# A chain of transformer blocks on one core, with the fillers of TensorE's waits taken out

## The chip, the cores and the metric

The kernel runs on one NeuronCore of a Trainium2 chip. It is written by hand for the five engines: TensorE (PE, matrix products; its weight loads are PEld), VectorE (DVE), ScalarE (ACT), GpSimd (POOL) and SyncE (SP, which issues the DMAs). The metric is the device time of one execution in microseconds (us), of which the median of some runs is taken. Changes under about 0.3% can't be told from none.

## The reference

Four blocks follow each other. Each takes the output of the last as x, of shape 4 x 512 x 256 (batch, sequence, width), and a context of the same shape. Cut to what is computed:

```python
# L0: 16 heads of 64, softmax over the QUERY axis, rows masked by mask[b, q]
q, k, v = x @ WQ.T + bQ, ctx @ WK.T + bK, ctx @ WV.T + bV
A = where(mask[:, None, :, None] == 0, -inf, q @ k^T / 8)
x0 = softmax(A, axis=2) @ v @ WO.T + bO + x
# L1: a gate from the pooled context, three iterations of which the last one counts, LayerNorm
# L2: 16 heads of 16, relu on Q, K, V, key mask and causal mask, relu on the output,
#     residual, normalised with the standard deviation over n - 1
# L3: self-attention (16 heads of 16, window of 64, linear bias by head), residual, LayerNorm;
#     cross-attention to ctx (no mask), residual, LayerNorm;
#     gelu(x @ w1 + b1) @ w2 + b2 (inner width 1024), residual, LayerNorm
```

## The kernel before, in words

A hardware loop runs over the four batch elements. One iteration computes all blocks for one element; I call the iterations b0 to b3. Every engine has its own program, and semaphores order them. Each engine runs its instructions in the order written, so a wait holds up all that is behind it on that engine.

TensorE writes into a ring of three PSUM slots of two banks (`ring`) and into `obank`, two banks for the products of probabilities and values. All uses of the ring stand in one list of jobs, `JOBS`; `start(name)` waits until the slot of the job has been drained, and the last matmul of a job increments `filled`. Who drains (VectorE or ScalarE) increments `drained`.

The jobs of an iteration that matter here, in TensorE's order:

- `V0`, `QK0`, `S0`: the 16 heads of 64 of block L0 (lines 1060 to 1088), then its output product (L1144) and block L1 (`tp`, `gate`, `agree`, with the matmuls of one column L1206 and the gate products L1162).
- `VC` (L1041): values of the cross-attention. Then `X1`: `turn(1)` transposes the normalised tiles `nat_n` (L1116), four tiles of two transposes. A tile is ready when VectorE has normalised it (L833, semaphores `tile_normed` and `norm_ready`). ScalarE drains the slot into `act_t` (L630 or L633).
- `Q2` (L1029), then `meanV` (L1222, sixteen matmuls of one column) and `meanO` (L1229).
- `attention(CAUSAL)` and its output product `O2` (L1327).
- `X2`, then `KS`, `QS` (L1029), `VS` (L1041), `attention(BANDED)`, `KC`, `OS`.
- `X3`, then `QC` (L1029), `attention(FULL)`, `OC`.
- `X4`, then `F1` (L1029) and `F2` (L1050). A product of 128 rows and 512 columns in fp32 is one instruction of the program and two in the trace, so F1 has 32 there.

An attention works on four groups of four heads. In the pass A (`pass_a`, L1251, for CAUSAL and BANDED with mask products L1237) scores are made with the queries on the partitions, and VectorE takes their maxima (L912). `turn_maxima` (job `T`, L1298) turns the maxima of a group, and ScalarE copies them into the query tiles (L673, two copies). Then pass B (L1268) makes the scores with the keys on the partitions, ScalarE takes the exponentials (L681), and `values` (L1287) multiplies them into `obank`. The first eight A passes of group 0 come before everything else; `group_steps` interleaves all that follows.

The query and key tiles of an attention are stacked by small DMAs, 24 for the keys (L381) and 24 for the queries (L388), which SyncE issues one after the other. The first pass A waits for the stacked tiles of its group (L1246). Before the queries are stacked, VectorE drains the projection in halves (L902), ScalarE rounds each (`high_q`, L623) and VectorE subtracts (L905). For the keys GpSimd makes the lower parts (`split_k`, L507).

Between the real work stand calls of `keep_warm(n)` (L1022). Each issues n products of two constants that stay in SBUF, a 128x128 identity and 512 columns, in bf16, into bank 0 of `obank` at times when that bank holds nothing. Nobody reads them, and they wait for nothing of their own. They stand behind the start of X1 (12), X2, X3 and X4 (18 each), behind each of these four (5), at the start of an attention (6), behind each of the eight first passes of FULL (2), behind the first eight passes (8), and before the first pass B (6): 162 in one iteration.

## Time and profile before

| | us |
|---|---|
| median of 3 runs | 1832.75 (1827.45 to 1833.13) |
| the profiled execution | 1834.59 |
| its span | 1832.5 |
| TensorE busy | 1615.1 (88%) |
| VectorE busy | 914.4 (50%) |
| ScalarE busy | 737.6 (40%) |
| GpSimd busy | 251.8 (14%) |

The span goes from the first to the last instruction of the profiled execution. Busy is the time in which an engine has an instruction under way; a matmul's record contains the time in which it passes through the array, so that records of neighbours overlap and a busy TensorE isn't one at its peak. "Granted clock" is the share of TensorE's full clock (2.4 GHz) that the chip let through; in a short stretch it is 1.00 or 0.50, and over a longer one the mean of both. In timelines, x12 is the number of instructions merged into one row, and the brackets hold the engine's idle time before them and what ended it.

### The profile page before, as it was taken

The numbers are of one execution on the slowest core, as the hardware profiler recorded it, in microseconds if no ns is written. First come the engines' busy times: TensorE is split into PE (matmuls) and PEld (weight loads), VectorE is DVE, ScalarE is ACT, GpSimd is POOL, SyncE is SP. The second block draws the span as 40 slices with busy tenths as digits, with TensorE's granted clock in tenths as the row PEclk, the third lists the DMA queues.
The fourth block names the chain that finished last, engine by engine and source line by source line (L and its number), as shares of the span: only waits on it lengthen the run. The fifth ranks groups of instructions, "written<-read, shape, count | busy, mean of one in ns | idle before, by whom it ended". The sixth has DMA issues, their size and how long they took to land.

```text
span 1832.5 us, 27225 instructions
## 1 busy us (share of the span) xinstructions
PE 1615.1 (88%) x9568; PEld 834.5 (46%) x9568; DVE 914.4 (50%) x2244; ACT 737.6 (40%) x1281; POOL 251.8 (14%) x116
## 2 busy tenths in 40 slices
PE   5999888888999988878999998887899999988786
PEld 2346445424435645532533554553253355545234
DVE  2653644472464474447166346445625635644561
ACT  1651434164264252417236316142724632514362
POOL 1012211201102121110110312111011031112102
PEclk9998998889999898889999989889999998988899
DMA  9001203402100211240210030224111013031300
GB/s 324 1 6 35 35 17 55 104 1 109 48 1 7 41 30 32 39 104 1 110 47 1 7 57 14 49 54 72 36 75 47 1 21 55 2 62 41 60 24 12
DMA packets 44869, 84.17 MB, mean 46 GB/s; under 512 B 10417, under 2 KB 28593, under 8 KB 44465
## 3 DMA queue, kind: packets, MB, share of 16 engines
q1 hardware_dynamic: 44288, 78.42, 18.2%
q10 hardware_dynamic: 432, 3.83, 0.5%
q8 instruction: 86, 1.41, 0.3%
q14 instruction: 63, 0.51, 0.1%
HBM read 42.37 MB, written 2.10 MB: 24 GB/s over the span
## 4 chain that ended last, share of the span: by engine, by line
PE 55%; issue 24%; DVE 8%; ACT 5%; POOL 4%; SPq 3%; DMA 1%; ACTq 0%; DVEq 0%; POOLq 0%
PE ring L1078 7%; PE obank L1088 7%; PE ring L1068 6%; PE ring L1029 5%; DVE nmax L912 4%; PE obank L1022 4%; PE ring L1144 3%; PE obank L1287 3%; PE ring L1327 3%; PE ring L1251 2%; SPq L381 2%; PE ring L1050 2%; ACT region_e L681 2%; PE ring L1268 2%; POOL q_all L528 2%
## 5 line engine op out<-in xcount | busy, mean ns | idle before, releaser
L912 DVE TENSOR_REDUCE nmax<-ring 128x2 f32<-128x1024 f32 (+4 forms) x384 | 318.2, 855 | 208.0 <-PE ring L1237 143.1
L681 ACT ACTIVATE region_e<-ring 128x1024 f32<-128x1024 f32 (+4 forms) x384 | 269.2, 732 | 140.9 <-PE ring L1237 87.3
L788 DVE CUSTOM_DVE_ANT_0 region_d<-ring,maskb 128x512 f32<-128x512 f32 x256 | 165.9, 687 | 101.1 <-issue 101.1
L605 ACT ACTIVATE region_e<-region_d,nmin 128x512 f32<-128x512 f32 x256 | 182.6, 714 | 81.8 <-DVE nmin L788 80.2
L673 ACT ACTIVATE q_all<-ring 2x1024 fp32r<-2x1024 bf16 x96 | 97.5, 1016 | 244.3 <-PE ring L1298 243.7
L1022 PE MATMUL obank<-cbf 128*128 128x512 bf16 x648 | 173.8, 412 | 0.0
L1237 PE MATMUL ring<-cbf 64*128 64x128 bf16 (+1 forms) x2048 | 168.2, 251 | 0.0
L1251 PE MATMUL ring<-k_tiles_a,q_all 64*128 64x512 f32 (+4 forms) x384 | 86.3, 457 | 65.5 <-DMA q_all<-q_parts 54.3
L1078 PE MATMUL ring<-region_q 64*128 64x512 f32 x512 | 126.1, 613 | 5.4 <-ACT region_q L594 5.4
L539 POOL TENSOR_TENSOR nat_x<-nat_n,rows 128x1024 f32<-128x1024 f32 x16 | 37.6, 2352 | 671.6 <-DVE nat_n L833 507.8
L1088 PE MATMUL obank<-region_e,vs 128*64 128x512 f32 x512 | 124.0, 605 | 0.0
L1251 PE MATMUL ring<-k_tiles_b,q_all 64*128 64x512 f32 (+4 forms) x384 | 81.9, 423 | 24.1 <-ACT q_all L673 15.1
L1022 PEld LDWEIGHTS obank<-cbf 128*128 128x128 bf16 x648 | 62.7, 103 | 82.6 <-issue 30.3
L1268 PE MATMUL ring<-q_all,k_tiles_a 64*128 64x512 f32 (+4 forms) x384 | 82.9, 427 | 18.7 <-DVE nmax L912 12.9
L1251 PEld LDWEIGHTS ring<-k_tiles_a,q_all 64*128 64x128 f32 x384 | 43.0, 221 | 103.7 <-DMA q_all<-q_parts 51.7
L1268 PE MATMUL ring<-q_all,k_tiles_b 64*128 64x512 f32 (+4 forms) x384 | 75.6, 412 | 13.1 <-ACT q_all L673 8.5
L1327 PE MATMUL ring<-w_out,region_d 128*128 128x256 f32 x384 | 85.7, 381 | 0.0
L514 POOL TENSOR_TENSOR q_all<-zero 128x2048 fp32r<-128x2048 f32 x8 | 28.6, 3598 | 404.0 <-DVE region_c L779 404.0
L1078 PEld LDWEIGHTS ring<-region_q 64*128 64x128 f32 x512 | 44.3, 186 | 84.8 <-issue 72.2
L1287 PE MATMUL obank<-region_e,region_b 128*32 128x192 f32 (+4 forms) x1024 | 81.7, 397 | 1.2 <-ACT region_e L681 0.8
L1287 PE MATMUL obank<-region_e,region_c 128*32 128x512 f32 x512 | 74.2, 654 | 7.0 <-ACT region_e L681 7.0
L983 DVE TENSOR_TENSOR nat_y<-ring,nat_x 128x512 f32<-128x512 f32 x16 | 11.1, 692 | 138.9 <-PE ring L1050 123.2
(169 smaller groups left out, 2260.9 us busy)
## 6 DMA issues: line engine op xcount, KB each, us to landing
q_all<-q_parts SPq DMA_DIRECT2D x288, 64.0 KB, 2.3
k_tiles_a<-k_parts SPq DMA_DIRECT2D x144, 64.0 KB, 2.3
k_tiles_b<-k_parts SPq DMA_DIRECT2D x144, 64.0 KB, 2.3
region_b<-in_w_f SPq DMA_DIRECT2D x8, 1024.0 KB, 5.2
wvo<-in_wv SPq DMA_DIRECT2D x4, 1024.0 KB, 7.8
wqk<-in_wq SPq DMA_DIRECT2D x4, 1024.0 KB, 11.0
wqk<-in_wk SPq DMA_DIRECT2D x4, 1024.0 KB, 12.9
wvo<-in_wo SPq DMA_DIRECT2D x4, 1024.0 KB, 5.4
```

Of the source, the lines that this page charges most:

```text
L605: ins = act.activation(e0[:, n % E0, h, :], sm0[:, n % 2, h, :], ACT.Exp, bias=nmin0[:, n, h:h + 1], scale=-1.0, accum_out=sum0[:, n, h:h ...
L681: act.activation(e16[:, n % 4, 2 * u:2 * u + 2, 0:nq], slot((a, "B", g, kt, u))[:, :, 0:nq], ACT.Exp)\
L788: ins = dve.tensor_tensor_reduce(out=sm0[:, n % 2, h, :], in0=slot(("S0", p, kt))[:, h, :], in1=maskb[:, :], scale=-1.0, scalar=3.0e38, op ...
L912: dve.tensor_reduce(nmax[:, qt, 2 * u:2 * u + 2], slot(name)[:, :, 0:nk], AX.X, ALU.max, negate=True)\
L1022: pe.matmul(obank[:, 0, :], cb("ident", P), cb("keyrows", S), start=True, stop=True)
L1078: ins = pe.matmul(dst[:, h, :], qk0[own, p % 2, 1, kt * P:(kt + 1) * P], qk0[own, p % 2, 0, :], start=True, stop=True)
L1088: ins = pe.matmul(obank[DK0 * h:DK0 * (h + 1), p % 2, :], vs0[:, n % 4, h, :], e0[:, n % E0, h, :], start=(kt == 0), stop=(kt == NT - 1))
L1237: ins = pe.matmul(dst[:, i, lo:lo + n], cb("halves", P, own, at=half * P), cb(table, n, own, at=half * whole + at), start=False, stop=(hal ...
L1251: ins = pe.matmul(dst[:, i, 0:nk], q_tiles[g][own, u, qt * P:(qt + 1) * P], k_tiles[g][own, u, k0:k0 + nk], start=True, stop=(a == FULL))
L1268: ins = pe.matmul(dst[:, i, 0:nq], k_tiles[g][own, u, kt * P:(kt + 1) * P], q_tiles[g][own, u, q0:q0 + nq], start=True, stop=(a == FULL))
L1287: ins = pe.matmul(obank[32 * s:32 * s + 32, (PAIRS + o) % 2, q0:q0 + nq], v_of[a][:, kt, h, :], e16[:, n % 4, s, 0:nq], start=(kt == 0), s ...
L1327: ins = pe.matmul(dst[j][:, i, 0:D], oT[:, t, m * P:(m + 1) * P], w_out[a][:, t, :], start=(t == 0), stop=(t == GROUPS - 1))
```

## The change

All calls of `keep_warm` and the function itself are deleted.

```diff
--- before.py
+++ after.py
@@ -1016,11 +1016,6 @@
                     pe.wait_ge(*free_for(name, b))
                     return slot(name)
 
-                def keep_warm(n):
-
-                    for _ in range(n):
-                        pe.matmul(obank[:, 0, :], cb("ident", P), cb("keyrows", S), start=True, stop=True)
-
                 def project(name, w, src, tiles):
 
                     dst = start(name)
@@ -1105,8 +1100,6 @@
                 def turn(n, src):
 
                     dst = start(("X", n))
-                    if n:
-                        keep_warm(12 if n == 1 else 18)
                     for m in range(NT):
                         if n and m + 1 < NT:
                             pe.wait_ge(tile_normed, (b * 5 + n - 1) * (NT - 1) + m + 1)
@@ -1209,7 +1202,6 @@
                 pe.wait_ge(k_loaded["lc"], 64)
                 project_nat("VC", w_sq["cv"], ctx_t)
                 turn(1, nat_n)
-                keep_warm(5)
                 pe.wait_ge(*drained_by(("X", 1), b))
                 project(("Q2",), w_sq["q2"], act_t, range(DT))
 
@@ -1299,20 +1291,14 @@
                     ins.then_inc(*ends_fill(name))
 
                 def attention(a):
-                    keep_warm(6)
                     for qt in range(NT):
                         for u in range(2):
                             pass_a(a, 0, qt, u)
-                            if a == FULL:
-                                keep_warm(2)
-                    keep_warm(8)
                     if a == BANDED:
                         pe.wait_ge(*drained_by(("VS", 1), b))
                         pe.wait_ge(ones_ready, b * 2 + 2)
                     for g in range(GROUPS):
                         for kind, *which in group_steps(g):
-                            if kind == "B" and which == [0, 0, 0]:
-                                keep_warm(6)
                             if kind in "ABTV":
                                 {"A": pass_a, "B": pass_b, "T": turn_maxima, "V": values}[kind](a, *which)
 
@@ -1335,7 +1321,6 @@
 
                 pe.wait_ge(k_loaded["ls"], 64)
                 turn(2, nat_n)
-                keep_warm(5)
                 pe.wait_ge(*drained_by(("X", 2), b))
                 project(("KS",), w_sq["sk"], act_t, range(DT))
                 project(("QS",), w_sq["sq"], act_t, range(DT))
@@ -1345,13 +1330,11 @@
                 project(("KC",), w_sq["ck"], ctx_t, range(DT))
                 out_heads(BANDED, "OS")
                 turn(3, nat_n)
-                keep_warm(5)
                 pe.wait_ge(*drained_by(("X", 3), b))
                 project(("QC",), w_sq["cq"], act_t, range(DT))
                 attention(FULL)
                 out_heads(FULL, "OC")
                 turn(4, nat_n)
-                keep_warm(5)
                 pe.wait_ge(*drained_by(("X", 4), b))
                 pe.wait_ge(k_loaded["ff"], b * 32 + 32)
                 for j in range(FT // 2):
```

No other instruction changes, so on TensorE each real instruction moves up by the fillers that stood ahead of it. Three places show it. Line numbers below 1016 stay, later ones fall by 5 to 18.

First TensorE between the values of the cross-attention and Q2. Before (L1022 are fillers, L1116 the transposes X1, L1029 is Q2; ISA and REGISTER_ALU rows are the computed waits):

```order
L1022 MATMUL obank<-cbf 128x512 x12
L1112 ISA
L1116 MATMUL ring<-ident,nat_n 128x128 x2
L1112 REGISTER_ALU
L1116 MATMUL ring<-ident,nat_n 128x128 x2
L1112 REGISTER_ALU
L1116 MATMUL ring<-ident,nat_n 128x128 x2
L1114 REGISTER_ALU
L1116 MATMUL ring<-ident,nat_n 128x128 x2
L1022 MATMUL obank<-cbf 128x512 x5
L1213 REGISTER_ALU
L1029 MATMUL ring<-act_t,w_q 128x512 x4
```

After (L1109 are the transposes, L1024 is Q2):

```order
L1036 MATMUL ring<-w_cv,ctx_t 128x256 x8
L1105 ISA
L1109 MATMUL ring<-ident,nat_n 128x128 x2
L1105 REGISTER_ALU
L1109 MATMUL ring<-ident,nat_n 128x128 x2
L1105 REGISTER_ALU
L1109 MATMUL ring<-ident,nat_n 128x128 x2
L1107 REGISTER_ALU
L1109 MATMUL ring<-ident,nat_n 128x128 x2
L1205 REGISTER_ALU
L1024 MATMUL ring<-act_t,w_q 128x512 x4
```

The transposes now stand right behind VC, and Q2 right behind the transposes.

Second TensorE from QC into the first A passes of FULL. Before (L1029 is QC, L1251 a pass A):

```order
L1029 MATMUL ring<-act_t,w_cq 128x512 x4
L1022 MATMUL obank<-cbf 128x512 x6
L1246 ISA
L1251 MATMUL ring<-k_tiles_a,q_all 128x512 x2
L1022 MATMUL obank<-cbf 128x512 x2
L1251 MATMUL ring<-k_tiles_a,q_all 128x512 x2
L1022 MATMUL obank<-cbf 128x512 x2
L1016 REGISTER_ALU
L1251 MATMUL ring<-k_tiles_a,q_all 128x512 x2
L1022 MATMUL obank<-cbf 128x512 x2
```

After (L1024 is QC, L1243 a pass A):

```order
L1024 MATMUL ring<-act_t,w_cq 128x512 x4
L1238 ISA
L1243 MATMUL ring<-k_tiles_a,q_all 128x512 x4
L1016 REGISTER_ALU
L1243 MATMUL ring<-k_tiles_a,q_all 128x512 x6
L1016 REGISTER_ALU
```

The passes stand behind each other with nothing between them but their waits for a drained slot.

Third TensorE at the end of FULL's first passes, up to the first pass B. Before (L1298 turns the maxima, L1268 is the first pass B):

```order
L1022 MATMUL obank<-cbf 128x512 x10
L1016 REGISTER_ALU
L1251 MATMUL ring<-k_tiles_a,q_all 128x512 x4
L1294 REGISTER_ALU
L1298 MATMUL ring<-cbf,mcol 128x128 x8
L1016 REGISTER_ALU
L1251 MATMUL ring<-k_tiles_a,q_all 128x512 x4
L1022 MATMUL obank<-cbf 128x512 x6
L1268 MATMUL ring<-q_all,k_tiles_a 128x512 x2
```

After (L1290 turns the maxima, L1260 is the first pass B):

```order
L1243 MATMUL ring<-k_tiles_a,q_all 128x512 x4
L1286 REGISTER_ALU
L1290 MATMUL ring<-cbf,mcol 128x128 x8
L1016 REGISTER_ALU
L1243 MATMUL ring<-k_tiles_a,q_all 128x512 x4
L1260 MATMUL ring<-q_all,k_tiles_a 128x512 x2
```

What stood between the eighth pass and the next, and between the last pass A and the first pass B, is gone. VectorE's, ScalarE's and SyncE's instructions are the same in both kernels.

## Rows read from the trace of the kernel before

**Rows 1.** View of the cores.
```profile
core 0: 1832.5 us, clock 0.937
```

**Rows 2.** The chain that ended last, by engine.
```profile
PE 55%; issue 24%; DVE 8%; ACT 5%; POOL 4%; SPq 3%; DMA 1%; ACTq 0%; DVEq 0%; POOLq 0%
```

**Rows 3.** Groups by cost: names, shapes, count, busy us, mean ns, idle before.
```profile
L1022 PE MATMUL obank<-cbf 128*128 128x512 bf16 x648 | 173.8, 412 | 0.0
```

**Rows 4.** Timeline of VectorE, X1 of b1: start us, us, what.
```profile
624.98 1.38 DVE L833 TENSOR_SCALAR nat_n<-nat_y,mv,std 128x256 f32<-128x256 f32 x4 [0.60 <-ACT std L643]
```

**Rows 5.** Timeline of TensorE, X1 of b1.
```profile
627.55 2.75 PE L1022 MATMUL obank<-cbf 128*128 128x512 bf16 x12
630.13 1.04 PE L1116 MATMUL ring<-ident,nat_n 128*128 128x128 f32 x8
```

**Rows 6.** Timeline of TensorE, X2 of b1.
```profile
707.18 1.65 PE L1116 MATMUL ring<-ident,nat_n 128*128 128x128 f32 x8 [1.98 <-DVE nat_n L833]
708.63 2.34 PE L1022 MATMUL obank<-cbf 128*128 128x512 bf16 x5
```

**Rows 7.** Timeline of ScalarE, X2 of b1.
```profile
708.87 1.02 ACT L630 ACTIVATE act_t<-ring 128x1024 f32<-128x1024 f32 x1 [2.61 <-PE ring L1116]
```

**Rows 8.** Timeline of TensorE before a first B: FULL b0, BANDED b1, FULL b2.
```profile
370.32 2.74 PE L1022 MATMUL obank<-cbf 128*128 128x512 bf16 x6
...
738.72 2.74 PE L1022 MATMUL obank<-cbf 128*128 128x512 bf16 x6
...
1275.23 1.47 PE L1022 MATMUL obank<-cbf 128*128 128x512 bf16 x6
```

**Rows 9.** Timeline of ScalarE at the same three places.
```profile
368.47 2.04 ACT L673 ACTIVATE q_all<-ring 2x1024 fp32r<-2x1024 bf16 x2 [20.78 <-PE ring L1298]
...
737.55 2.04 ACT L673 ACTIVATE q_all<-ring 2x1024 fp32r<-2x1024 bf16 x2 [17.96 <-PE ring L1298]
...
1273.46 2.04 ACT L673 ACTIVATE q_all<-ring 2x1024 fp32r<-2x1024 bf16 x2 [20.42 <-PE ring L1298]
```

**Rows 10.** Timeline of VectorE, first passes of FULL in b0.
```profile
357.99 1.23 DVE L912 TENSOR_REDUCE nmax<-ring 128x2 f32<-128x1024 f32 x1 [0.47 <-PE ring L1251]
359.68 6.88 DVE L912 TENSOR_REDUCE nmax<-ring 128x2 f32<-128x1024 f32 x6 [0.47 <-PE ring L1251]
```

**Rows 11.** Timeline of TensorE, first pass of FULL in b0.
```profile
355.46 0.80 PE L1251 MATMUL ring<-k_tiles_a,q_all 64*128 64x512 f32 x2 [7.92 <-DMA q_all<-q_parts]
```

**Rows 12.** Timeline of TensorE, X4 and F1 of b0.
```profile
435.77 1.41 PE L1116 MATMUL ring<-ident,nat_n 128*128 128x128 f32 x8
...
438.72 14.00 PE L1029 MATMUL ring<-act_t,region_b 128*128 128x512 f32 x32 [0.46 <-ACT act_t L633]
```

**Rows 13.** Timeline of TensorE, gate products of b1 at full and half clock.
```profile
607.74 1.13 PE L1162 MATMUL ring<-w_gt,region_q 128*128 128x256 f32 x4
...
614.54 2.08 PE L1162 MATMUL ring<-w_gt,region_q 128*128 128x256 f32 x4
```

**Rows 14.** Stretches, first pass to output product: CAUSAL b0, b1; FULL b0, b2.
```profile
core 0: us, PE busy (x) PEld busy (x) DVE busy (x) ACT busy (x) POOL busy (x), PEclk, DMA share, GB/s
193.38:252.41 59.03, 53.19 (x592) 30.50 (x591) 38.38 (x66) 29.73 (x40) 14.12 (x7) 0.97 0.12 21
643.55:701.16 57.61, 51.75 (x592) 29.84 (x592) 38.37 (x66) 29.79 (x40) 14.13 (x7) 1.00 0.12 21
...
355.46:431.88 76.42, 65.87 (x350) 25.30 (x351) 49.66 (x61) 39.49 (x40) 0.00 (x0) 0.88 0.21 60
...
1260.79:1333.05 72.26, 61.38 (x351) 24.41 (x352) 49.58 (x61) 39.49 (x40) 0.00 (x0) 0.95 0.22 64
```

**Rows 15.** Stretches from FULL's first pass while at half clock, b1 and b2.
```profile
808.03:813.80 5.77, 5.77 (x14) 1.55 (x14) 3.67 (x3) 0.00 (x0) 0.00 (x0) 0.50 0.58 101
...
1260.79:1264.40 3.61, 3.61 (x10) 1.07 (x10) 2.31 (x2) 0.00 (x0) 0.00 (x0) 0.50 0.61 104
```

**Rows 16.** Timeline of SyncE, query DMAs of FULL in b0.
```profile
349.93 15.14 SPq L388 DMA_DIRECT2D q_all<-q_parts  x24
```

**Rows 17.** Timeline of ScalarE, upper halves of FULL's queries in b0.
```profile
347.07 0.63 ACT L623 ACTIVATE q_parts<-region_e 128x512 fp32r<-128x512 f32 x1 [1.08 <-DVE region_e L902]
```

## The prediction

> **What bounds the kernel now.** First the view of cores: 1832.5 us, mean granted clock 0.937 [rows 1]. TensorE is granted either 2.4 or 1.2 GHz, so the share s of the span at 1.2 GHz follows from 1 - s/2 = 0.937: s = 0.126, about 231 us. Then the chain of waits by engine [rows 2]: 55% of the span is TensorE's own work, no other engine has more than 8%, and 24% is "issue", where the chain follows an engine that waits for nothing shown. So TensorE's stream is the backbone. Third, the groups by cost: the fillers are 648 matmuls, 173.8 us of busy time, with no idle time before them [rows 3]; 162 stand in each of the four loop iterations, which I call b0 to b3. Last, the timelines around each place with fillers. They sort the fillers into those that end before the next operand is there (free) and those that outlast it (paid). What both kinds may also do is keep the clock up.
>
> **What the removal gives back on the path.**
> (a) X1. The last tile of nat_n is ready at 626.36 (start 624.98 plus 1.38) [rows 4], before the twelve fillers start at 627.55; the transposes start behind them, at 630.13 [rows 5]. Nothing else is late then: 2.58 us in each iteration, 10.3 us. X1, Q2, the query DMAs and the first pass hang on it in a row.
> (b) X2. In b1 the five fillers start at 708.63 at half clock and take to about 710.8 [rows 6], while ScalarE has drained X2 at 709.89 [rows 7]: 0.9 us. So in b1, b2 and b3: 2.8 us.
> (c) Before the first B of an attention, six fillers. In BANDED they start at 738.72 at half clock, 2.7 us [rows 8], and ScalarE's two copies of the maxima end at 739.59 [rows 9]: 1.8 us late, in three iterations. In FULL of b0 the copies end at 370.51 and the fillers at 373.0: 2.5 us. At full clock six fillers take 1.4 us, to 1276.6 against copies that end at 1275.50: 1.1 us, three times [rows 8, 9]. CAUSAL has no such overhang. Sum 5.4 + 2.5 + 3.3 = 11.2 us.
> (d) FULL's first eight passes. VectorE needs 1.13 us start to start (the last six take 6.88), but the reductions at 357.99 and 359.68 stand 1.69 apart with 0.47 idle [rows 10], since at half clock a pass and its two fillers take TensorE 1.7 us. A pass alone takes it 0.8 at most [rows 11], so VectorE will set the pace: two times 0.56, about 1.1 us in each iteration, 4.5 us.
> Together 28.8 us. The 18 fillers ahead of X2, X3 and X4 give nothing back. At X2 TensorE idles another 1.98 us behind them [rows 6]; at X4, and alike at X3, they end as the first tile comes, with no idle time before the transposes [rows 12]. The fillers ahead of FULL's first pass end 7.92 us before the DMA that it waits for [rows 11].
>
> **What it costs in clock.** Prices first. For dense fp32 work the cost is all of it: four L1162 matmuls take 1.13 us at full clock and 2.08 at half [rows 13], so each us at half clock does half a us of work. In the attention phases VectorE and ScalarE share the bound, and the same phase in different iterations gives the price [rows 14]: CAUSAL 59.03 us at clock 0.97 against 57.61 at 1.00 is 1.42 us for 3.5 us at half clock, 0.40; FULL 76.42 at 0.88 against 72.26 at 0.95 is 4.16 for 11.1, 0.37, which I take for BANDED too. How long half clock lasts once work is back: in the four starts of FULL it ended after 3.6 to 5.8 us (both ends shown) [rows 15], 4.4 on average. Taken for a dense place, that loses 2.2 us, with ends 1.8 and 2.9.
> (e) X2. Without fillers TensorE idles 18 x 0.215 + 1.98 = 5.9 us before the transposes, then another 1.3 for ScalarE. The clock fell there in b1 to b3 even with the 18 fillers. KS and QS, dense, start at half clock, and their end releases the split and the DMAs of BANDED's first pass. 2.2 us in each iteration, less some 0.3 that b1 to b3 pay already: 7.8 us, ends 6 and 11.
> (f) X3. Idle 3.9 us, transposes, idle 1.5, then QC at half clock, 2.2 us late. But SyncE issues 24 key DMAs first: it comes to the queries at 349.93 [rows 16], and their upper halves are ready at 347.70 [rows 17]. This slack of 2.2 us hides all but the upper end: 0 to 0.7, I take 0.3, in all 1.2 us. Were SyncE earlier, it would be the full 2.2 each time.
> (g) X4. The same pause, and behind it 32 dense F1 matmuls, 14.00 us [rows 12], with no slack, then F2 and the next iteration. 2.2 plus 0.2 for the last transposes: 9.6 us in all, ends 8 and 12.
> (h) The attention phases now begin at half clock: CAUSAL behind sixteen one-column matmuls and a wait for the query DMAs, BANDED and FULL behind waits for DMAs alone. The first passes hardly pay, since VectorE is their bound. Then come the turned maxima, a wait of 2.0 us for ScalarE's copies with nothing in it, and the first B steps, which pay the prices above. I put the added half-clock time that pays at 7 us in CAUSAL (none now in b1 to b3), 5 in BANDED and 6 in FULL: 7 x 0.40 + 5 x 0.37 + 6 x 0.37 = 6.9 us, 27.5 us in all. No row shows this size. Its ends: one short stretch of 3.5 us a phase, as CAUSAL of b0 has, 4.0 us an iteration, 16 us; or 11 us more in FULL, as much as b0 has over its best, and 9 in each other phase, 11 us an iteration, 44 us. Stretches recur inside FULL after the first, which keeps me off the low end.
> Sum: 7.8 + 1.2 + 9.6 + 27.5 = 46.1 lost, 28.8 won, 17.3 us slower. The profiled execution took 1834.6 us (2.1 around its span), 1.8 over the median of the three runs shown. 1834.6 + 17.3 - 1.8 = 1850 us, 0.9% slower.
>
> The Trainium skill ("TensorE: Matmul & The Clock Gate", Part 1) says: "For modeling, the ramp penalty is <1% of a typical kernel span". By that rule all clock cost here would stay under 18 us and the sum would come out at least 10 us faster, at 1822 us. The trace disagrees: 231 us at half clock [rows 1] times 0.37 is already 85 us, over 4% of the span.
>
> **Rivals.**
> Faster (0.10): in the attention phases half clock costs nothing, as VectorE and ScalarE hide it. Then (h) is zero: -28.8 + 18.6 = -10.2, 1822 us. For it: each of the two is busy for half of CAUSAL and FULL or more [rows 14]. Against it: the same rows, where the phase grows with its half-clock share while VectorE's time stays (49.66 and 49.58 us in FULL). It decides once (h) is under 5 us.
> The fillers don't hold the clock (0.02): half clock stays as it is and the 28.8 us alone go, 1804 us. For it: 231 us at half clock exist in spite of them. Against it: CAUSAL is at 1.00 in three iterations of four.
> No change (0.13): a short stretch per phase and X2 at its low end: -28.8 + 16.8 + 16 = +4, 1837 us. For it: in CAUSAL of b0 the clock came back after one stretch. Against it: FULL of b0.
> Much slower (0.15): the clock falls again and again once TensorE has less to do, (h) = 44, (e) to (g) at their upper ends: -28.8 + 44 + 11 + 2.8 + 12 = +41, 1874 us. For it: FULL of b0, at 0.88 where b2 has 0.95 with the same instructions. Against it: most of a phase never had fillers, so only its start changes.
> My forecast (0.60): 1850, its own range 1839 to 1863.
>
> **How the numbers follow.** A measurement of this kernel tells 0.3% (5.5 us) from no change, so "same" is 1827 to 1838. Faster 0.12 from the first two rivals; same 0.15, the third and the foot of my case; slower 0.73. The range for 8 in 10 takes in the no-change case and most of the way to the slowest: 1831 to 1869.
>
> **What would show it.** (a) is right if the transposes of X1 stand right behind the VC matmuls. (d) is right if FULL's first reductions run at 1.13 us. (g): F1's 32 matmuls take about 16.2 us. (f): FULL's first pass comes at most 0.7 us later behind BANDED's end. (h): CAUSAL takes 59 to 61 us from its first pass to the end of its output product, at a clock near 0.93, and the mean clock of the span falls to about 0.90. I am wrong if CAUSAL stays at 1.00, if F1 stays at 14.0 us, or if the phases don't grow with their half-clock share.

## The result: 0.6% slower

The changed kernel takes 1843.2 us (median of 8 runs, 1837.3 to 1848.7) against 1832.6 us for the kernel before in the same comparison: ratio 1.0059 [1.0037, 1.008]. The forecast was 1850 us, 0.9% slower. Profiled, it took 1843.0 us where the kernel before took 1834.6.

The view of cores, to be held against [rows 1]:

```profile
core 0: 1840.9 us, clock 0.873
```

The mean clock fell by more than expected (0.90 was said): 1 - s/2 = 0.873 gives 25.4% of the span at 1.2 GHz, 468 us against 231. So 237 us more at half clock cost 8.4 us net. The chain that ended last, by engine, against [rows 2]:

```profile
PE 59%; issue 16%; DVE 10%; ACT 6%; SPq 5%; DMA 2%; POOL 2%; ACTq 0%; DVEq 0%; POOLq 0%
```

Most of what "issue" lost lies in BANDED (190.6 us before, 64.9 after). There the chain of the kernel before follows GpSimd and finds nothing that released its instructions, so the two shares don't compare. The fillers stood on that chain as TensorE's own work, 3.5%; they are gone, VectorE went from 8 to 10% and SyncE from 3 to 5%. The list of what TensorE waited for shows where the fillers stood (engine, line, releaser: total us, times, longest):

```profile
PE ring L1243 <- DMA q_all<-q_parts: 67.1, 16, 6.9
PE ring L1109 <- DVE nat_n L833: 53.3, 12, 5.9
```

The second row is the three turns at X2, X3 and X4: 53.3 us in which TensorE now idles. In the kernel before the row had four waits, at X2 alone, of at most 2.0 us [rows 6].

The two timelines that the prediction named first. TensorE at X1 of b1 (start us, us, what), against [rows 5]:

```profile
623.57 2.33 PE L1036 MATMUL ring<-w_cv,ctx_t 128*128 128x256 f32 x9
625.74 1.04 PE L1109 MATMUL ring<-ident,nat_n 128*128 128x128 f32 x8
628.32 3.70 PE L1024 MATMUL ring<-act_t,w_q 128*128 128x512 f32 x8 [1.54 <-ACT act_t L633]
```

The transposes stand right behind the VC matmuls, and behind its pause of 1.54 us Q2 still runs at full clock (3.70 us for eight). TensorE at X2 and at X4 with F1, in b1, against [rows 6, 12]:

```profile
704.13 1.97 PE L1109 MATMUL ring<-ident,nat_n 128*128 128x128 f32 x8 [5.86 <-DVE nat_n L833]
707.21 5.49 PE L1024 MATMUL ring<-act_t,w_sk 128*128 128x512 f32 x6 [1.11 <-ACT act_t L630]
...
887.98 16.81 PE L1024 MATMUL ring<-act_t,region_b 128*128 128x512 f32 x32 [1.54 <-ACT act_t L633]
```

F1 went from 14.00 us to 16.81 (16.2 was said). At X2 the first matmuls of KS run at half clock, for 5.6 us and not 4.4. That stretch (its bounds, its length, the busy us of each engine, the granted clock, the DMA share, GB/s):

```profile
core 0: us, PE busy (x) PEld busy (x) DVE busy (x) ACT busy (x) POOL busy (x), PEclk, DMA share, GB/s
...
707.21:712.81 5.60, 5.60 (x7) 2.50 (x8) 0.00 (x0) 0.00 (x0) 0.00 (x0) 0.50 0.00 0
```

VectorE at FULL's first passes of b0, against [rows 10]:

```profile
356.43 9.14 DVE L912 TENSOR_REDUCE nmax<-ring 128x2 f32<-128x1024 f32 x8 [5.03 <-PE ring L1243]
```

Eight reductions in 9.14 us, 1.14 each and no idle between them, though TensorE is at half clock there: VectorE sets the pace, as (d) had it. Of the other signs, CAUSAL takes 59.3 us from its first pass to the end of its output product, inside the 59 to 61 that were said, but at a clock of 0.89 to 0.90 and not 0.93. FULL's first pass comes 0.2 to 1.1 us later behind BANDED's end, 0.6 on average, where at most 0.7 was said.

**Where the time went.** I cut each iteration at the same first instructions in both traces and summed each stretch over the four iterations. In us, with the part at half clock behind the slash:

| stretch | before | after | difference |
|---|---|---|---|
| start to end of VC | 637.2/54.6 | 635.5/47.8 | -1.7 |
| end of VC to X1's transposes | 9.7/0 | -0.7/0 | -10.4 |
| end of Q2 to CAUSAL's first pass | 28.4/13.7 | 27.6/18.4 | -0.8 |
| CAUSAL, first pass to first B | 42.3/0 | 43.4/29.7 | +1.1 |
| CAUSAL, first B to output product | 190.1/3.4 | 193.8/20.1 | +3.7 |
| X2's transposes to KS | 13.3/8.4 | 12.3/12.3 | -1.0 |
| KS to end of QS | 29.1/1.8 | 39.7/22.6 | +10.6 |
| BANDED, first pass to first B | 57.0/38.6 | 49.1/35.5 | -7.9 |
| BANDED, first B to output product | 192.7/35.9 | 203.0/71.4 | +10.3 |
| X3's transposes to QC | 11.8/0 | 13.0/10.1 | +1.2 |
| QC | 14.8/0 | 25.3/21.4 | +10.5 |
| end of QC to FULL's first pass | 37.0/16.6 | 27.7/18.0 | -9.3 |
| FULL, first pass to first B | 66.0/20.4 | 56.6/56.6 | -9.4 |
| FULL, first B to output product | 230.1/24.4 | 229.0/34.6 | -1.1 |
| X4's transposes to F1 | 11.8/0 | 14.0/14.0 | +2.2 |
| F1 | 56.0/0 | 67.1/22.4 | +11.1 |

The stretches left out differ by 0.7 us in all; the sum is the 8.4 us of the spans.

### The profile page after: what moved, and what is told of

The parts are those of the page before. It is cut to its first block, busy times and chain, and to the rows that moved or that the text cites. A ratio compares the mean times of both kernels' runs of the same rounds, so it can differ in the third digit from the quotient of the medians.

```text
span 1840.9 us, 25929 instructions
## 1 busy us (share of the span) xinstructions
PE 1534.9 (83%) x8920; PEld 822.3 (45%) x8920; DVE 913.6 (50%) x2244; ACT 739.4 (40%) x1281; POOL 251.8 (14%) x116
## 4 chain that ended last, share of the span: by engine, by line
PE 59%; issue 16%; DVE 10%; ACT 6%; SPq 5%; DMA 2%; POOL 2%; ACTq 0%; DVEq 0%; POOLq 0%
PE ring L1024 8%; PE ring L1073 7%; PE obank L1083 6%; PE ring L1063 6%; DVE nmax L912 5%; PE ring L1313 4%; PE obank L1279 4%; PE ring L1260 3%; PE ring L1137 3%; SPq L388 3%; PE ring L1243 2%; PE ring L1229 2%; PE ring L1045 2%; ACT region_e L681 2%; SPq L381 2%
## 5 line engine op out<-in xcount | busy, mean ns | idle before, releaser
L1229 PE MATMUL ring<-cbf 64*128 64x128 bf16 (+1 forms) x2048 | 191.4, 276 | 0.0
L673 ACT ACTIVATE q_all<-ring 2x1024 fp32r<-2x1024 bf16 x96 | 97.6, 1016 | 229.3 <-PE ring L1290 228.6
L1243 PE MATMUL ring<-k_tiles_a,q_all 64*128 64x512 f32 (+4 forms) x384 | 114.4, 599 | 81.4 <-DMA q_all<-q_parts 67.1
L1260 PE MATMUL ring<-q_all,k_tiles_a 64*128 64x512 f32 (+4 forms) x384 | 95.3, 489 | 25.7 <-DVE nmax L912 11.7
L1243 PEld LDWEIGHTS ring<-k_tiles_a,q_all 64*128 64x128 f32 x384 | 58.9, 301 | 115.0 <-DMA q_all<-q_parts 61.6
L1243 PE MATMUL ring<-k_tiles_b,q_all 64*128 64x512 f32 (+4 forms) x384 | 80.0, 413 | 24.5 <-ACT q_all L673 15.8
L1260 PE MATMUL ring<-q_all,k_tiles_b 64*128 64x512 f32 (+4 forms) x384 | 77.0, 418 | 13.3 <-ACT q_all L673 8.5
L983 DVE TENSOR_TENSOR nat_y<-ring,nat_x 128x512 f32<-128x512 f32 x16 | 11.1, 692 | 152.2 <-PE ring L1045 136.6
L1229 PEld LDWEIGHTS ring<-cbf 64*128 64x128 bf16 x2048 | 72.5, 114 | 28.3 <-issue 15.4
L1055 PE MATMUL ring<-wvo,ctx_t 128*128 128x512 f32 x128 | 59.0, 616 | 25.0 <-ACT kcol L576 18.8
L1260 PEld LDWEIGHTS ring<-q_all,k_tiles_a 64*128 64x128 f32 x384 | 46.0, 231 | 74.6 <-DVE nmax L912 31.7
```

Source lines behind the costliest of these rows:

```text
L1229: ins = pe.matmul(dst[:, i, lo:lo + n], cb("halves", P, own, at=half * P), cb(table, n, own, at=half * whole + at), start=False, stop=(hal ...
L1243: ins = pe.matmul(dst[:, i, 0:nk], q_tiles[g][own, u, qt * P:(qt + 1) * P], k_tiles[g][own, u, k0:k0 + nk], start=True, stop=(a == FULL))
L1260: ins = pe.matmul(dst[:, i, 0:nq], k_tiles[g][own, u, kt * P:(kt + 1) * P], q_tiles[g][own, u, q0:q0 + nq], start=True, stop=(a == FULL))
```

## The experiments

Each is the kernel before with the edit shown, unless it says otherwise. The times are medians, the ratios stand against runs of the kernel before on the same chip, with their 95% intervals. Sums "by place" are over four iterations and cut as in the table above.

**One place alone.** First X1 without its twelve and five:

```diff
-                        keep_warm(12 if n == 1 else 18)
+                        keep_warm(0 if n in (1,) else 12 if n == 1 else 18)
...
-                keep_warm(5)
```

> Only the 12 fillers ahead of X1 and the 5 behind it are gone. Theory A (every place pays or gains for itself, as the two traces compare place by place): the transposes move up by 2.6 us in each iteration, clock of Q2 unchanged, 10.3 us faster than before, about 1822 us. Theory B (the fillers of X1 also keep up the clock for Q2 and the passes behind it, so that their removal costs what it gives): within 4 us of before.

1813.9 us, ratio 0.9902 [0.9866, 0.9939], clock 0.949. By place, VC's end to X1 gave 10.4 us as (a) said. Most of the rest lies where no instruction was changed: BANDED's B steps were 6.6 us shorter, and the stretch up to the end of VC was 10.4 us shorter in the profiled execution (626.8 against 637.2, 27.3 at half clock against 54.6), and its runs spread from 1802.9 to 1824.1. That stretch takes longer the more half clock falls into it. The kernel after shows two cases (b0, then b1):

```profile
18.82:175.23 156.41, 153.78 (x556) 72.92 (x557) 80.94 (x289) 68.75 (x160) 19.00 (x6) 0.98 0.23 66
466.26:625.91 159.65, 155.03 (x557) 73.70 (x557) 85.57 (x305) 69.26 (x162) 23.80 (x8) 0.96 0.11 26
```

Same matmuls, 3.2 us apart. It isn't that b0 is the first: in the kernel without X1's fillers b1 to b3 have 6.8 us at half clock too and take 156.4 to 156.6. The stretches by place are therefore the sharper tool, and a single profiled total is none.

The 18 and the 5 at X2, X3 and X4 out, all else kept:

```diff
+                        keep_warm(0 if n in (2, 3, 4) else 12 if n == 1 else 18)
...
-                keep_warm(5)        (behind X2, X3 and X4)
```

> Only the fillers at X2, X3 and X4 (18 ahead and 5 behind each) are gone. Theory A: X2 with KS and QS 9.6 us slower over the four iterations, X3 to FULL's first pass 2.4, X4 with F1 13.3: together 25 us slower than before, about 1857 us. Theory B (a place's half clock goes on into the attention behind it): BANDED and FULL lengthen as well, 35 us or more. The forecast's own terms (e) to (g) would give 18.6 slower.

1846.3 us, ratio 1.0082 [1.0051, 1.0113]: slower as expected, by less. By place: X2's transposes to QS +7.0 us, X3's transposes to FULL's first pass -0.6, X4's to F1 +1.8, F1 +8.6, BANDED's first passes -3.7 and B steps +3.1. In the profiled execution part of what this loses is hidden, since the stretch before VC's end was again 11.3 us shorter.

X3 alone, and X4 alone:

> Only the 23 fillers at X3 are gone. Theory A (SyncE's queue of key DMAs covers QC): QC itself takes 10 us longer over the four iterations, the wait behind it shrinks by nearly as much, and FULL's first pass comes 0 to 1 us later behind BANDED's end in each iteration: 0 to 4 us slower than before. Theory C (no such cover): FULL's first pass comes 2.8 us later each time, 11 us slower.

```diff
+                        keep_warm(0 if n in (3,) else 12 if n == 1 else 18)
...
-                keep_warm(5)        (behind X3)
```

1834.5 us (12 runs), ratio 1.0006 [0.9981, 1.003]: no difference. Yet QC is not free of it. TensorE at X3 of b0 in this kernel:

```profile
342.51 1.62 PE L1116 MATMUL ring<-ident,nat_n 128*128 128x128 f32 x8 [3.73 <-DVE nat_n L833]
...
345.67 6.04 PE L1029 MATMUL ring<-act_t,w_cq 128*128 128x512 f32 x8 [1.54 <-ACT act_t L633]
```

QC took 6.04 us instead of 3.70; over four, 23.9 against 14.8. The wait from its end to FULL's first pass shrank from 37.0 to 27.6 us in exchange: from X3's transposes to the first pass it is 64.6 against 63.6, +1.0. SyncE's key DMAs cover it, as (f) argued. They can because the twelve ahead of the queries took 8.4 to 8.7 us in the kernel before. In the mix below they take 7.6 and the same stretch is 59.9 us, so there the 64.6 would be 4.7 more: X3's fillers are worth nothing here and may be worth some 5 us where the key DMAs are shorter. No run drops them there.

> Only the 23 fillers at X4 are gone. Theory A: F1's 32 matmuls take 16.8 instead of 14.0 us and the transposes with ScalarE's drain 3.5 instead of 2.9, nothing covers it: 13 us slower in the stretch from the transposes to F1's end. The forecast's size (4.4 us of half clock) would give 2.4 an iteration, 9.6.

```diff
+                        keep_warm(0 if n in (4,) else 12 if n == 1 else 18)
...
-                keep_warm(5)        (behind X4)
```

1849.2 us, ratio 1.0081 [1.0053, 1.011]. By place X4's transposes to F1 +2.2, F1 +9.8: 12.0 us, against the 9.6 of (g). TensorE in b0:

```profile
434.79 1.97 PE L1116 MATMUL ring<-ident,nat_n 128*128 128x128 f32 x8 [3.73 <-DVE nat_n L833]
...
438.30 16.88 PE L1029 MATMUL ring<-act_t,region_b 128*128 128x512 f32 x32 [1.54 <-ACT act_t L633]
```

**Is it enough that TensorE is busy?** At X4 the fillers became products of one column, so that TensorE is kept issuing and streams almost nothing:

```diff
-                        keep_warm(12 if n == 1 else 18)
+                        if n == 4:
+                            for _ in range(17):
+                                pe.matmul(obank[:, 0, 0:1], ident[:, :], ones[:, 0:1], start=True, stop=True)
+                        else:
+                            keep_warm(12 if n == 1 else 18)
...
-                keep_warm(5)
+                for _ in range(5):
+                    pe.matmul(obank[:, 0, 0:1], ident[:, :], ones[:, 0:1], start=True, stop=True)
```

> At X4 the 18 and 5 fillers of 512 columns are replaced by 17 and 5 products of one column in fp32 (44 records of about 0.11 us), which keep TensorE's queue occupied for about as long, 3.8 and 1.1 us, with hardly any column streamed. Theory D (what holds the clock is the columns streamed): half clock at F1 as without fillers, F1 at 16.8 us, 13 us slower than before in that stretch. Theory E (it is enough that TensorE executes something): F1 stays at 14.0 us and the stretch as before.

1848.4 us, ratio 1.0071 [1.0046, 1.0095]: as slow as without any. TensorE in b0 (each product is two matmuls in the trace):

```profile
431.05 4.26 PE L1111 MATMUL obank<-ones,ident 128*128 128x1 f32 x34
435.17 1.95 PE L1120 MATMUL ring<-ident,nat_n 128*128 128x128 f32 x8
436.91 2.13 PE L1359 MATMUL obank<-ones,ident 128*128 128x1 f32 x10
438.90 16.79 PE L1029 MATMUL ring<-act_t,region_b 128*128 128x512 f32 x32
```

No idle time stands before any of these rows, TensorE counts as busy throughout, and F1 begins at half clock all the same: 16.79 us. So a busy engine in the profile is no sign that the clock will hold. These products differ from the fillers in width, in type and in their operands, and no run separates these. The small products also outlasted their wait by 0.5 us per iteration (1.9 in all), which is in the total.

**The attention phases.** All their fillers out, those at X1 to X4 kept. This is (h) against (c) and (d) alone:

```diff
-                    keep_warm(6)
+                    keep_warm(0 if a in (0, 1, 2) else 6)
...
-                                keep_warm(2)
-                    keep_warm(8)
+                                pass
+                    keep_warm(0 if a in (0, 1, 2) else 8)
...
-                                keep_warm(6)
+                                keep_warm(0 if a in (0, 1, 2) else 6)
```

> Only the fillers in the three attentions are gone. Theory A: CAUSAL 4.0 us slower, BANDED 2.4 slower, FULL 10.5 faster by the comparison of the traces: 4 us faster than before, about 1828.5. The forecast's term (h) of 27.5 against gains of 14 to 16 would make it 12 us slower.

1814.6 us, ratio 0.9912 [0.9883, 0.994]. By my forecast (27.5 lost, 15.7 won) it should have been 12 us slower; it is 17 us faster. By place: CAUSAL +7.0 (first pass to first B +2.7, B steps +4.3); BANDED's first passes -4.3, B steps -5.3; FULL's first passes -9.4, B steps +1.1; also the wait ahead of FULL's first pass -3.7 and X2 to QS -3.8, since here the clock did not fall at X2. With the same 18 fillers there it fell in 13 of 28 iterations of seven kernels, in none of this one's four. CAUSAL's clock did fall as I expected, to 0.94 in its B steps (b0):

```profile
202.68:251.43 48.75, 45.06 (x496) 26.44 (x498) 29.54 (x52) 27.89 (x38) 7.57 (x4) 0.94 0.01 3
```

It cost 1.1 us an iteration in the B steps and 0.7 before them, not 2.8. This run refutes (h) as sized, though part of its gain (X2 to QS -3.8, the start to VC's end -4.5) comes from places whose fillers it kept.

BANDED needs care. In the five kernels that keep its fillers and X2's 18 (the one before, and those without X1's, X3's and X4's or with one column at X4), its first passes sum to 51.3 to 57.3 us and its B steps to 186.1 to 200.2. So a difference there from one profile, up to some 6 and 14 us, can come with no edit near it.

X1's and the attention phases' fillers out, X2 to X4 kept:

> Only the fillers at X2, X3 and X4 are left. Theory A: the gain at X1 (10.3) and that in the attentions (4) add: 14 us faster than before, 1818 us. Theory B (the removals interact, since the clock that one place leaves behind is what the next begins with): the sum fails by more than 6 us, to 1825 or over.

1810.1 us, ratio 0.9876 [0.984, 0.9912]: 21 us faster, more than theory A's 14, and theory B is refuted as stated. The medians of the two removals alone (17 and 17 us) don't add either. By place the parts do: VC's end to X1 -10.4, FULL's first passes -9.4, CAUSAL +5.2. With no loss at X3 alone and 15 us at X4 alone, the fillers that pay stand ahead of X4 and, as the next run shows, of X2.

**Does BANDED inherit the clock?** The changed kernel (after), with fillers given back at X2 alone, 27 ahead, for all of the wait, and 5 behind:

```diff
+                    if n == 2:
+                        keep_warm(27)
...
                 turn(2, nat_n)
+                keep_warm(5)
```

> The changed kernel with fillers at X2 alone: 27 ahead and 5 behind. Theory A (a place pays for itself): KS and QS at full clock, 11 to 13 us from X2 to QS's end, BANDED as in the changed kernel (203 us from its first pass B to its output product, over four iterations): about 1831 us. Theory B (BANDED inherits the clock that KS and QS leave): BANDED falls to about 190 us as in the kernels that keep the fillers at X2 and have none in the attentions, together 24 us faster than the changed kernel, 1819 us.

1825.5 us (12 runs), ratio to the kernel before 0.9956 [0.9932, 0.9979], where after has 1.0059 [1.0037, 1.008]: about 1.0% or 19 us for one place; the spans differ by 19.7. The place itself, X2's transposes to the end of QS, gives 13.4 (38.6 against 52.0, none of it at half clock). BANDED gives 8.2 more (243.9 against 252.1): 12.5 in its B steps, of which its first passes give 4.3 back. The time lies between the two theories. After, b0 and b1, then this kernel, b0 and b1:

```profile
286.88:335.77 48.89, 43.87 (x504) 30.46 (x504) 22.05 (x47) 22.72 (x42) 9.93 (x5) 0.87 0.24 57
737.62:788.62 51.00, 46.42 (x504) 32.19 (x504) 22.04 (x47) 23.13 (x42) 9.93 (x5) 0.81 0.22 55
```

```profile
284.97:330.95 45.98, 41.21 (x504) 28.62 (x504) 22.04 (x47) 22.70 (x42) 9.91 (x5) 0.94 0.25 61
732.20:778.19 45.99, 41.17 (x504) 28.62 (x504) 22.04 (x47) 22.70 (x42) 9.91 (x5) 0.94 0.25 61
```

Same 504 matmuls, same VectorE and ScalarE time; 3 to 5 us less with the higher clock. In b3, though, they took 51.1 us here too, so this gain doesn't come every time. Other kernels make chance alone unlikely: six keep X2's fillers and have none in BANDED, and in their 24 iterations this stretch took 47.3 us on average, above 48.8 in four; in after it took 48.9 to 51.7 in all four. So dropping X2's fillers probably cost more than X2 itself. Two things stay open. The medians don't tell it, since 19 us less the place's 13.4 leaves 5.5, with an interval about as wide. And that KS and QS hand their clock on isn't shown: in the kernel without the fillers at X2, X3 and X4 they are at half clock for 17.4 us, and BANDED, with its own fillers, has less half clock in its B steps than before (30.8 against 35.9 us).

**A better mix.** None at X1, 27 ahead of X2 so that they last to its operand, 18 at X3 and X4, CAUSAL's kept, none in BANDED and FULL:

```diff
-                        keep_warm(12 if n == 1 else 18)
+                        keep_warm({1: 0, 2: 27, 3: 18, 4: 18}[n])
...
-                keep_warm(5)        (behind X1 only)
...
-                    keep_warm(6)
+                    keep_warm(0 if a in (1, 2) else 6)
...         (the 2 out, the 8 and the last 6 likewise)
```

> Fillers only where they cover a wait ahead of dense work or ahead of CAUSAL's steps: none at X1, 27 instead of 18 ahead of X2 (the wait there is 5.9 us), 18 at X3 and X4, 5 behind X2 to X4, those of CAUSAL kept, none in BANDED and FULL. By places: X1 10.3 faster, X2 with KS and QS 4 faster (all at full clock), CAUSAL as before, BANDED's and FULL's starts 8 and 9 faster: about 30 us faster than before, 1802 us, if the rest of the phases stays. Theory B (phases inherit the clock state and lose it again) would leave less than 20.

1796.9 us, ratio 0.981 [0.978, 0.9839], the lowest median of all: 37 us under the kernel before, and 46 under the changed one's median, which is from another comparison. About 30 us under the kernel before was expected, so theory B is out. TensorE at X2 of b1, against [rows 6]:

```profile
690.32 4.05 PE L1022 MATMUL obank<-cbf 128*128 128x512 bf16 x18
694.41 1.41 PE L1116 MATMUL ring<-ident,nat_n 128*128 128x128 f32 x8
695.65 1.24 PE L1022 MATMUL obank<-cbf 128*128 128x512 bf16 x5
696.93 3.70 PE L1029 MATMUL ring<-act_t,w_sk 128*128 128x512 f32 x8
```

(The window begins within the 27, hence 18.) No idle time, and no half clock in KS and QS, in this and all 20 iterations of the five kernels with 27; the last five take 1.24 us where they took 2.34 at half clock. By place against before: X1 -10.4, X2 to QS -3.8, BANDED's first passes -5.0 and B steps -4.4, the wait ahead of FULL -3.7, its first passes -9.4, B steps +1.0, CAUSAL with the wait ahead of it +2.5. Another -4.6 lies in the stretch up to VC's end, which has no fillers in any kernel.

**Three changes to the mix.** Four fillers back ahead of the first B of BANDED and FULL, in the hope that they fit into the wait for the copies:

```diff
-                                keep_warm(0 if a in (1, 2) else 6)
+                                keep_warm(4 if a in (1, 2) else 6)
```

> The mix with 4 fillers ahead of the first pass B of BANDED and FULL: at half clock they take 1.7 us and end before ScalarE's copies of the maxima (2.0 us). Theory F (half clock in the first steps of an attention costs 0.1 to 0.25 us per us, as 40 iterations of the ten kernels show, and the later stretches come by themselves): 0 to 4 us faster than the mix. Theory G (the first steps pay 0.37 like the rest, as the forecast had it): they return to full clock some 3 to 5 us earlier in eight places, 10 us or more faster than the mix.

1812.1 us, ratio 0.9893 [0.9866, 0.9919]: slower than the mix, where neither theory had it. They don't fit. TensorE, then ScalarE, before FULL's first B in b0 (one filler's record is missing from the trace):

```profile
365.80 1.49 PE L1022 MATMUL obank<-cbf 128*128 128x512 bf16 x3 [0.33 <-ACT q_all L673]
367.21 0.80 PE L1267 MATMUL ring<-q_all,k_tiles_a 64*128 64x512 f32 x2
```

```profile
363.71 2.04 ACT L673 ACTIVATE q_all<-ring 2x1024 fp32r<-2x1024 bf16 x2 [18.84 <-PE ring L1297]
```

The copies end at 365.75, TensorE's last pass A at 365.47; at half clock four fillers last to 367.2. That is 1.3 us in each FULL phase (61.9 against 56.6 over four) and 3.0 over four in BANDED. The stretch before FULL's first B is at 0.50 with and without them. Behind it they do act: in six of the eight phases full clock is back within 1.9 us of the first B, where the mix needs 5.4 to 9.2. But in all six the clock falls again later in the phase, once or more. BANDED's B steps even came out 10.0 us longer, at 45.2 us of half clock against 36.2; whether that belongs to the fillers or to chance isn't settled by one profile.

CAUSAL's own fillers out of the mix, and only the six ahead of its first pass out:

> The mix without CAUSAL's 20 fillers. Theory F: first pass to first B 10.6 to 10.8..11.3 us, first B to the output product 47.2 or 48.6 to 48.5, at most 1.9 us an iteration, 4 to 7 us slower than the mix. Theory G: 2.8 us an iteration as in the forecast, 11 us slower.

> The mix without the 6 fillers ahead of CAUSAL's first pass. In the mix they ended after the query DMAs, at half clock: from Q2's end to the first pass 30.0 us over four iterations against 27.7 without. Theory A: that stretch 2.3 us shorter, the rest as in the mix, 1 to 3 us faster than it, about 1795. Theory B (they also set the clock of CAUSAL's passes): first pass to output product longer by up to 4 us, so no gain, or a loss of 2 us.

```diff
-                    keep_warm(0 if a in (1, 2) else 6)
+                    keep_warm(0)
...     (the first of the two also without the 8 and the last 6)
```

1803.2 us, 0.9847 [0.9821, 0.9874], and 1805.2 us, 0.9839 [0.9798, 0.988]; the mix has 0.981 [0.978, 0.9839]. Both intervals meet the mix's, so neither is told from it. By place they trade: without any, CAUSAL's B steps lose 3.6 us and the wait ahead of its first pass wins 2.3.

## Why the forecast was right in sign and too high

The forecast was 17.3 us slower; the spans of the two profiled executions differ by 8.4, the medians by 10.6. The steps as the prediction put them, over four iterations of the profiled executions:

| step | forecast | measured |
|---|---|---|
| (a) X1 | -10.3 | -10.4 |
| (c), (d) first passes of BANDED and FULL | -15.7 | -17.3 |
| (b), (e) X2, KS and QS | +5.0 | +9.6 |
| (f) X3 and QC | +1.2 | +2.4 |
| (g) X4 and F1 | +9.6 | +13.3 |
| (h) attention phases | +27.5 | +14.0 |
| stretches that should not move | 0 | -3.2 |
| sum | +17.3 | +8.4 |

**What the fillers held up (a, c, d): right in mechanism.** For FULL the two terms said 10.3 us and 9.4 came. For BANDED (c) said 5.4 and 7.9 came, but its first passes took 57.0 us in the kernel before and 51.3 to 57.3 in others with the same fillers, so that part may be luck. FULL's first passes to its first B take 14.2 us in all four iterations, against 15.8 to 17.5, though they are at half clock from end to end:

```profile
1263.51:1277.67 14.16, 9.84 (x32) 4.22 (x33) 13.22 (x14) 2.03 (x2) 0.00 (x0) 0.50 0.45 79
```

VectorE is busy 13.22 of 14.16 us, and that is why TensorE's clock costs nothing there. TensorE before the first B of b0, against [rows 8, 9], now waits 0.44 us for the copies instead of making them wait:

```profile
368.52 0.80 PE L1243 MATMUL ring<-k_tiles_a,q_all 64*128 64x512 f32 x2 [0.34 <-DVE nmax L912]
369.75 0.79 PE L1260 MATMUL ring<-q_all,k_tiles_a 64*128 64x512 f32 x2 [0.44 <-ACT q_all L673]
```

**The dense places (b, e, g): mechanism right, size too small.** The price was right: over 56 iterations of fourteen kernels, KS and QS, QC and F1 grow by 0.49 us for each us at half clock. The term that missed was "how long half clock lasts once work is back", 4.4 us, taken from starts of FULL; in the changed kernel it lasted 5.6 us in KS, 5.5 to 5.7 in F1 and 5.0 to 5.7 in QC. The kernel without the fillers at X2, X3 and X4 alone had 2.8 to 6.2, on average 4.1, so the profile of the changed kernel may stand at the long end by chance.

**(f): cover right, rest doubled.** QC lost 10.5 us and 9.3 came back out of the wait. SyncE in b1:

```profile
794.21 7.58 SPq L381 DMA_DIRECT2D k_tiles_b<-k_parts  x12
...
803.83 8.32 SPq L388 DMA_DIRECT2D q_all<-q_parts  x13
```

```profile
803.17 0.63 ACT L623 ACTIVATE q_parts<-region_e 128x512 fp32r<-128x512 f32 x1 [2.08 <-DVE region_e L902]
```

The keys are issued by 801.79 and the upper halves of the queries are ready at 803.80: SyncE waited 2 us for them. The slack of 2.2 us [rows 16, 17] was used up; what QC lost (2.8 us here) and the 0.6 us by which it started later exceed it. The twelve key DMAs took 7.6 us instead of 8.4 (see the last section), which gained nothing here, since SyncE waited for the queries anyway.

**(h): the failed step.** Half of it stood. I assumed 18 us an iteration of added half clock that pays, 72 in all, and the B steps of the three phases have 62.4 more (16.7 in CAUSAL, 35.5 in BANDED, 10.2 in FULL; I had 28, 20 and 24). The price failed: I took 0.37 to 0.40 from whole phases [rows 14], and the 62.4 us cost 12.9, that is 0.21. The stretches that the change adds lie at the start, while those in [rows 14] lie mostly in the middle (of FULL's 11.1 us, 3.7 lie in its first passes). CAUSAL's B steps show both at nearly the same length: before b0 with one stretch in the middle, before b1 with none, after b1 with one at the start:

```profile
203.94:252.57 48.63, 44.41 (x497) 25.54 (x498) 29.48 (x52) 27.70 (x38) 7.57 (x4) 0.96 0.02 4
...
654.14:701.32 47.18, 42.99 (x497) 24.88 (x498) 29.45 (x52) 27.76 (x38) 7.57 (x4) 1.00 0.02 3
```

```profile
649.79:698.27 48.48, 44.68 (x496) 25.98 (x496) 29.45 (x52) 27.89 (x38) 7.57 (x4) 0.95 0.01 2
```

3.4 us in the middle cost 1.45 (0.42 a us); 5.0 us at the start cost 1.3 (0.26). Other iterations repeat it: eleven with one middle stretch of 3.4 us take 48.6 to 48.7 us, twenty with one of 4.7 to 6.1 us at the start take 48.4 to 48.8, and those without any 47.2. In FULL the start stretch often also took the place of later ones. After b1 as a whole and its first 8.8 us, then before b0 and b2:

```profile
823.44:880.75 57.31, 48.61 (x288) 20.03 (x288) 36.27 (x48) 37.51 (x38) 0.00 (x0) 0.92 0.17 62
...
823.44:832.24 8.80, 8.29 (x36) 3.50 (x36) 6.21 (x7) 5.05 (x5) 0.00 (x0) 0.50 0.01 2
```

```profile
373.00:432.04 59.04, 49.73 (x290) 19.99 (x290) 35.30 (x47) 37.46 (x38) 0.00 (x0) 0.91 0.16 60
1276.63:1333.21 56.58, 46.94 (x290) 19.38 (x290) 35.60 (x48) 37.46 (x38) 0.00 (x0) 0.97 0.17 63
```

After has its 8.8 us in one piece and none behind it, and takes 57.3 us; b0 of before has 0.5 us at the start and three later pieces of 3.4, and takes 59.0. Against 55.4 us, which FULL's B steps took in one iteration without any half clock (the kernel without X4's fillers), that is 0.22 and 0.33 a us. BANDED came nearest to my price (10.3 us for 35.5, 0.29), with the scatter named above; there, too, before b0 and b2, at 0.5 and 17.1 us of half clock, stand 0.44 apart.

```profile
291.11:335.87 44.76, 39.50 (x506) 26.80 (x506) 22.05 (x47) 22.70 (x42) 9.91 (x5) 0.99 0.24 58
1189.10:1241.22 52.12, 44.69 (x505) 30.38 (x506) 22.05 (x47) 23.10 (x42) 9.91 (x5) 0.84 0.23 55
```

Why a start stretch is cheaper was not taken apart. In the first passes it is VectorE's bound; behind the first B it may be that VectorE still has passes A to reduce, which stays an argument.

So the total of 1850 owes something to errors of both signs: (h) was 13.5 us too high, the dense places with X3 9.5 too low, and 4.9 came from the rest, 3.2 of it from stretches with nothing changed. 10.3 of the 14.0 us of (h) are BANDED's B steps. In the two kernels that drop the attention fillers but keep X2's 18, the same four stretches of (h) grow by 2.8 and 3.6 us in all. So its size hangs on what happens at X2, and with one profile of each kernel on BANDED's scatter; in every case it is well under 27.5.

**The rivals.** "Faster", half clock costs nothing in the attention phases, fails for this change: (h) is 14 us, over its threshold of 5. With X2's fillers kept it comes near, as (h) is 2.8 us there, and the kernel without the attention fillers is faster than before, which I had at +12. "The fillers don't hold the clock" falls with X4 and with the mix at X2. "Much slower" falls: in the changed kernel FULL's B steps hold one piece of half clock in each iteration, where before they hold one to four. "No change" had +4 (1837 us): the median of 1843.2 lies half way between it and my 1850, and the 8.4 us of the spans are nearer to it than to my 17.3. The Trainium skill says that the ramp penalty is "<1% of a typical kernel span" ("TensorE: Matmul & The Clock Gate", Part 1). That sentence stands beside counts of slow matmuls at a kernel's start, and I stretched it in the prediction to all clock cost. So taken it does not hold here: F1, QC and KS with QS alone lose 32 us (1.7% of the span) to half clock.

## What to carry to other kernels

A filler pays only where it lasts until the operand comes and not longer, and where dense TensorE work stands on the path behind it: here X4, and X2, where 18 kept the clock in 15 of 28 iterations and 27 in all 20. Price half clock by stretch, not by phase: 0.5 us a us in dense fp32 work, 0.05 or nothing where VectorE is the bound, 0.2 to 0.4 in between and least at a phase's start. Look at both ends of each wait before you fill it, since a filler at half clock takes twice its time and starts only when the queue ahead of it is done.

## What the runs showed that I had not expected

I had counted the six fillers ahead of FULL's first pass as free since they end 7.9 us before the DMA [rows 11]. In the kernels without them the wait from QC's end to that pass was 8.3 to 8.4 us, wherever QC itself was at full clock; in those with them, 8.8 to 9.5. What became shorter is SyncE's issue of keys. Before, and in the mix (b1):

```profile
794.09 8.38 SPq L381 DMA_DIRECT2D k_tiles_b<-k_parts  x12
```

```profile
777.80 7.56 SPq L381 DMA_DIRECT2D k_tiles_b<-k_parts  x12
```

In the 56 iterations of the fourteen kernels the twelve took 8.0 to 8.7 us in the 16 in which a packet of the instruction queue started with them or while they were issued, and 7.5 to 7.6 us in the other 40. The six needn't be what brings it there: the kernels without them lack all fillers in BANDED and FULL, and without X3's 23, the six kept, there was no such packet in seven of eight iterations. Whether the packet stalls SyncE, and what puts it there, stays open.

Half clock also comes and goes far from any edit. The stretch up to the end of VC, without fillers in any kernel, takes mostly about 156.5 us with 6.8 at half clock or 159.5 with 13.7; the sum over four iterations was 637.2 in the kernel before, 626.8 without X1's fillers and 632.6 in the mix. Up to 11 us of a total can come from there. That may be why the kernel without X1's fillers gained 17 us for a place worth 10.4.
